# Neighbour sums with two matmuls per tile, eight-tile groups and 48 tiles per loop turn; locations on ScalarE's queue, t values added on GpSimd

## What is computed

```python
def sage(x, src, dst, W_l, b, W_r):
    summed = segment_sum(x[src], dst, N)
    deg = segment_sum(ones(E), dst, N)
    return (summed / maximum(deg, 1)[:, None]) @ W_l + b + x @ W_r

h = relu(sage(x, ..., W1_l, b1, W1_r))
x = x + sage(h, ..., W2_l, b2, W2_r)
```

## Time and profile before

| | us |
|---|---|
| time, median of 3 runs | 11395.62 |
| lowest and highest run | 11379.77, 11412.15 |
| span of the profiled execution | 11414.2 |
| PE, PEld busy | 6127.3 (54%), 4965.7 (44%) |
| DVE busy | 5543.8 (49%) |
| ACT busy | 2324.9 (20%) |
| POOL busy | 6528.7 (57%) |
| mean granted TensorE clock | 0.602 |

### The profile page before, as it was taken

One profiled execution on the slowest core, in us unless ns is written; L12 is line 12 of the kernel. 1 busy time (PEld: TensorE's weight loads), 2 busy tenths in 40 slices (PEclk: granted clock), 3 DMA queues, 4 the chain that ended last, 5 costly groups with the idle time before them and its releaser, 6 DMA issues. The chain is left out here.

```text
span 11414.2 us, 177920 instructions
## 1 busy us (share of the span) xinstructions
PE 6127.3 (54%) x45373; PEld 4965.7 (44%) x45374; DVE 5543.8 (49%) x10403; ACT 2324.9 (20%) x6224; POOL 6528.7 (57%) x6578
## 2 busy tenths in 40 slices
PE   5200066665777766666554646555555555554655
PEld 1100035553666664544444434334444444443444
DVE  9300075555555548888763536741111333383535
ACT  0000024442333321111004050011111111125050
POOL 0677737775677777777406060047777777756060
PEclk9555587787555558787556565565555555556565
DMA  9960012221433321111737475662000111126465
GB/s 367 199 61 5 14 44 84 82 83 50 117 102 101 100 73 51 53 54 49 145 94 246 84 261 127 140 52 27 13 13 8 27 28 28 25 53 255 98 252 104
DMA packets 1406964, 1074.85 MB, mean 94 GB/s; under 512 B 959771, under 2 KB 1258287, under 8 KB 1395302
## 3 DMA queue, kind: packets, MB, share of 16 engines
q1 hardware_dynamic: 1012260, 637.37, 24.3%
q0 software_dynamic: 239808, 283.02, 8.0%
q10 hardware_dynamic: 154752, 152.84, 4.4%
HBM read 553.89 MB, written 595.41 MB: 101 GB/s over the span
## 5 line engine op out<-in xcount | busy, mean ns | idle before, releaser
L2507 POOL DMA_INDIRECT msg<-msg,idx x1792 | 1743.1, 973 | 585.8 <-issue 531.7
L2337 POOL DMA_INDIRECT cell<-rec,idx x1008 | 1003.3, 995 | 1027.4 <-ACT rec L2325 737.0
L666 DVE TENSOR_TENSOR oh<-iota_f,rd 128x512 bf16<-128x512 f32 (+1 forms) x1261 | 824.8, 692 | 1379.1 <-PE ps L2259 1083.6
L979 POOL DMA_INDIRECT run_rows<-rec,idx x704 | 728.7, 1035 | 1274.7 <-ACT rec L962 1105.5
L2061 POOL DMA_INDIRECT cell<-rec,idx x1008 | 1073.6, 1065 | 421.3 <-issue 305.8
L1738 POOL DMA_INDIRECT rec_d<-rec,idx x880 | 907.2, 1031 | 453.8 <-issue 266.5
L397 POOL DMA_INDIRECT rec_r<-sc_rec,sc_idx x832 | 816.2, 981 | 596.5 <-ACT sc_rec L388 317.4
L2487 PE MATMUL ps<-w_stn,hft 128*128 x1792 | 600.1, 494 | 397.6 <-ACT hft L2441 389.6
L2274 PE MATMUL ps<-h_rows,oht 128*128 x2016 | 481.6, 403 | 583.3 <-ACT oht L2281 582.9
L1053 PE MATMUL ps<-got,oh 128*128 128x33 bf16 x12096 | 599.0, 197 | 334.7 <-DVE oh L666 319.0
L948 PE MATMUL ps<-planes,hot 128*128 x5632 | 493.2, 265 | 516.1 <-ACT rec L962 406.9
(11 more groups left out here) (416 smaller groups left out, 13529.0 us busy)
## 6 DMA issues: line engine op xcount, KB each, us to landing
loc<-loc_s SPq DMA_DIRECT2D x88, 2048.0 KB
got<-run_rows SPq DMA_DIRECT2D x1008, 112.0 KB
got<-rec_d SPq DMA_DIRECT2D x252, 416.0 KB
rec_d<-padd ACTq DMA_DIRECT2D x4, 13312.0 KB
rec_d<-padd ACTq DMA_DIRECT2D x4, 12896.0 KB
cell<-rec,idx POOLq DMA_INDIRECT x2016
loc<-loc_d SPq DMA_DIRECT2D x252, 128.0 KB
cin<-cell SPq DMA_DIRECT2D x224, 136.0 KB, 2.2
```

What stands on the lines that cost most here:

```text
L666: return nc.vector.tensor_tensor(oh, bcast(iota_f[:, :].unsqueeze(1), [P, G, P]), bcast(local.unsqueeze(2), [P, G, P]), ALU.is_equal)
L979: nc.gpsimd.indirect_dma_start(out=out, out_offset=bass.IndirectOffsetOnAxis(ap=idx[:, u, m % HU:m % HU + 1], axis=0), in_=rec[:, m, :], i ...
L2337: nc.gpsimd.indirect_dma_start(out=cells, out_offset=bass.IndirectOffsetOnAxis(ap=idx[:, n, g:g + 1], axis=0), in_=rec[:, n, g, :], in_off ...
L2507: nc.gpsimd.indirect_dma_start(out=msgs, out_offset=bass.IndirectOffsetOnAxis(ap=idx[:, n, g:g + 1], axis=0), in_=msg[:, n, g, :], in_offs ...
```

## The change

`sum_runs` is written anew with groups of GS = 8 tiles and RING = 6 buffers, so a turn has 48 tiles and there are 21 turns. The hi and mid planes lie side by side in a row, and one matmul of 66 columns takes both; a second of 33 adds lo to the first half. A block has 66 columns in PSUM, seven blocks to a bank, seven banks (`PER_BANK2`, `ABANKS2`), and the two halves are added when they are copied out. The addresses come from a new map `db`, made in `psum_address`, and are loaded 24 at a time, twice a turn. In the t pass the locations are loaded from ScalarE's queue when the pick six groups back is done; the pick stands in front of its own group's sum tiles and has one bank, 7; VectorE makes both one-hots three groups ahead and keeps only the here sum; GpSimd adds the three parts of t of the source side and both sides to the coordinates, four operations a group. `sort_sp` stores the map `db` without loading it; `source_runs` loads it. Parts that only rename or follow from this are cut.

```diff
+        def psum_address(then, c, tb, to, sets):
+
+            up = c["up"]
+            per, banks = (PER_BANK2, ABANKS2) if sets == 2 else (PER_BANK, ABANKS)
+            then(nc.vector.tensor_scalar(up[:, :], tb[:, :], float(per), None, ALU.is_ge))
+            for q in range(2, banks):
+                then(nc.vector.scalar_tensor_tensor(out=up[:, :], in0=tb[:, :], scalar=float(q * per), in1=up[:, :],
+                                                    op0=ALU.is_ge, op1=ALU.add))
+            then(nc.vector.tensor_scalar(up[:, :], up[:, :], float(512 - per * sets * AW), None, ALU.mult))
+            then(nc.vector.scalar_tensor_tensor(out=up[:, :], in0=tb[:, :], scalar=float(sets * AW), in1=up[:, :],
+                                                op0=ALU.mult, op1=ALU.add))
+            then(nc.vector.tensor_copy(to[:, :], up[:, :]))
...
+            elif tag == "r":
+                psum_address(then, c, tb, c["tba"], 2)
+            elif tag == "d":
+                psum_address(then, c, tb, c["tba"], 1)
+                psum_address(then, c, tb, c["tbb"], 2)
...
+            GS = 8
+            RING = 6
+            TURNS = TILES_D // (GS * RING)
+            HALF_TURN = RING // 2
+            K = TURNS * RING
+            PAIR = 2 * AW
...
-                        with sp.Fori(0, NID) as i:
-                            for n in range(R):
-                                k, t = i * R + n, i * STEP + n * G
+                        with sp.Fori(0, TURNS) as i:
+                            for n in range(RING):
+                                k = i * RING + n
                                 if planes is not None:
-                                    sp.wait_ge(s_node, k + 1)
-                                    sp.dma_start(loc[:, n, :], bcast(loc_d[ds(t * P, G * P)].unsqueeze(0), [P, G * P])).then_inc(s_loc[n], 16)
                                     sp.wait_ge(s_there, k + 1)
                                 sp.wait_ge(s_sum, k + 1)
-                                sp.dma_start(got[:, n, :, :], view[:, ds(t, G), :]).then_inc(s_got[n], 16)
+                                sp.dma_start(got[:, n, :, :], view[:, ds(k * GS, GS), :]).then_inc(s_got[n], 16)
...
+                        for q in range(ABANKS2):
+                            b0, nb = q * PER_BANK2, min(PER_BANK2, NB - q * PER_BANK2)
+                            nc.scalar.copy(table[:, q * 512:q * 512 + nb * PAIR].rearrange("p (b w) -> p b w", w=PAIR)[:, :, 0:12],
                                            planes[:, b0:b0 + nb, 3 * AW:3 * AW + 12]).then_inc(s_table, 1)
+                        with act.Fori(0, TURNS) as i:
+                            for n in range(RING):
+                                k = i * RING + n
+                                act.wait_ge(s_pick, k + 1)
+                                nc.scalar.dma_start(loc[:, n, :], bcast(loc_d[ds(k * GS * P, GS * P)].unsqueeze(0),
+                                                                        [P, GS * P])).then_inc(s_loc[n], 16)
...
-                            for g in range(G):
-                                mm = nc.tensor.matmul(ps[:, 6 + n % 2, g * 12:(g + 1) * 12], node_hot[:, n, g * P:(g + 1) * P],
-                                                      table[:, ds(at[g], 12)], start=True, stop=True)
-                            mm.then_inc(s_pick, 1)
...
+                        with pe.Fori(0, TURNS) as i:
+                            for n in range(RING):
+                                k, of = i * RING + n, n % HALF_TURN * GS
+                                if n % HALF_TURN == 0:
+                                    at = block_ids(ENG.PE, "db", k * GS, ABANKS2 * 512 - PAIR, HALF_TURN * GS)
+                                if planes is not None:
+                                    pe.wait_ge(s_node, k + 1)
+                                    pe.wait_ge(s_here, k + 1)
+                                    for g in range(GS):
+                                        mm = nc.tensor.matmul(ps[:, 7, g * 12:(g + 1) * 12],
+                                                              node_hot[:, n, g * P:(g + 1) * P], table[:, ds(at[of + g], 12)],
+                                                              start=True, stop=True)
+                                    mm.then_inc(s_pick, 1)
...
-                                for g in range(G):
-                                    for q in range(3):
-                                        mm = nc.tensor.matmul(sums[:, ds(at[n * G + g], AW)], oh[:, n, g, :], part[n][:, g, q * AW:(q + 1) * AW],
-                                                              start=False, stop=False)
+                                for g in range(GS):
+                                    nc.tensor.matmul(sums[:, ds(at[of + g], PAIR)], oh[:, n, g, :], part[n][:, g, 0:PAIR],
+                                                     start=False, stop=False)
+                                    mm = nc.tensor.matmul(sums[:, ds(at[of + g], AW)], oh[:, n, g, :], part[n][:, g, PAIR:PAIR + AW],
+                                                          start=False, stop=False)
...
+                        def hots(i, n):
+                            k = i * RING + n
+                            if planes is not None:
+                                v.wait_ge(s_loc[n], 16 * (i + 1))
+                                v.wait_ge(s_pick, k + 1)
+                                nc.vector.tensor_scalar(node_hot[:, n, :], loc[:, n, :], lane_c[:, 0:1], None, ALU.is_equal).then_inc(s_node, 1)
+                            v.wait_ge(s_sum, k + 1)
+                            nc.vector.tensor_tensor(oh[:, n, :, :], bcast(iota_f[:, :].unsqueeze(1), [P, GS, P]),
+                                                    bcast(rd[:, ds(k * GS, GS), LOC].unsqueeze(2), [P, GS, P]), ALU.is_equal).then_inc(s_hot, 1)
...
+                        def keep_here(i, n):
+                            k = i * RING + n
+                            v.wait_ge(s_pick, k + 1 + RING)
+                            v.wait_ge(s_with, k + 1)
+                            nc.vector.tensor_reduce(here[:, n, :, :],
+                                                    ps[:, 7, 0:GS * 12].rearrange("p (g q f) -> p g f q", g=GS, q=3)[:, :, 0:KD, :],
...
+                            AHEAD = 3
+
+                            def turn(i, last):
+                                for n in range(RING):
+                                    keep_here(i, n)
+                                    if not last or n + AHEAD < RING:
+                                        hots(i + (n + AHEAD) // RING, (n + AHEAD) % RING)
...
+                        for q in range(ABANKS2):
+                            nb = min(PER_BANK2, NB - q * PER_BANK2)
+                            nc.vector.tensor_copy(acc[:, q * PER_BANK2:q * PER_BANK2 + nb, :],
+                                                  ps[:, q, 0:nb * PAIR].rearrange("p (b w) -> p b w", w=PAIR)[:, :, 0:AW]).then_inc(s_kept, 1)
+                        for q in range(ABANKS2):
+                            nb = min(PER_BANK2, NB - q * PER_BANK2)
+                            to = acc[:, q * PER_BANK2:q * PER_BANK2 + nb, :]
+                            v.wait_ge(s_kept, q + 1)
+                            nc.vector.tensor_tensor(to, to, ps[:, q, 0:nb * PAIR].rearrange("p (b w) -> p b w", w=PAIR)[:, :, AW:PAIR],
+                                                    ALU.add).then_inc(s_kept, 1)
...
+                            for n in range(RING):
+                                k = i * RING + n
+                                new, att = (rd[:, ds(k * GS, GS), w:w + KD] for w in (NEWP, ATT))
+                                pool.wait_ge(s_got[n], 16 * (i + 1))
+                                pool.wait_ge(s_new, k + 1)
+                                nc.gpsimd.sem_inc(tick, 1)
+                                hi, mid, lo = (part[n][:, :, 3 * AW + 4 * q:3 * AW + 4 * q + KD] for q in range(3))
+                                nc.gpsimd.tensor_tensor(there[:, n, :, :], hi, mid, ALU.add).then_inc(s_part, 1)
+                                pool.wait_ge(s_part, k + 1 + RING)
+                                nc.gpsimd.sem_inc(tick, 1)
+                                nc.gpsimd.tensor_tensor(there[:, n, :, :], there[:, n, :, :], lo, ALU.add).then_inc(s_there, 1)
+                                pool.wait_ge(s_here, k + 2)
+                                nc.gpsimd.sem_inc(tick, 1)
+                                nc.gpsimd.tensor_tensor(new, here[:, n, :, :], att, ALU.add).then_inc(s_with, 1)
+                                pool.wait_ge(s_with, k + 1 + RING)
+                                pool.wait_ge(s_there, k + 1 + RING)
+                                nc.gpsimd.sem_inc(tick, 1)
+                                nc.gpsimd.tensor_tensor(new, new, there[:, n, :, :], ALU.subtract).then_inc(s_new, 1)
```

(2 more changed lines are left out.)

154 lines of the change are left out of this document (51 added, 103 removed).

## The result

The changed kernel takes **11179.13 us** (median of 5 runs, 11169.43 to 11236.53), the kernel before in the same session 11395.85 (5 runs). The ratio is 0.9823, with a 95% interval of 0.9807 to 0.9838: 217 us less by the medians. The forecast was 11166, 230 less.

What follows compares the result with a forecast made beforehand. TensorE's instruction queue was taken to bound the plain passes. Plain passes -117, t pass -141, ends +22, t pass start and end +4 and address map +2 gave -230 from 11395.6, so 11166 us; range 11110 to 11280.

Steps and rivals of the forecast that it cites:

- What bounds: Plain passes: TensorE's instruction queue sets the pace; a tile's address takes 0.115 us whether one matmul follows or three.
- The matmul rival: Sum passes: matmuls set the tile's step after all, so dropping one saves 109 us more, kernel 11057; chance 0.10.
- Plain passes, -117: Three plain sum passes: a turn of 10.25 us, 21 turns 215 us against 254.3, so -39 each.
- hand-over between groups: TensorE's queue: time from one group of tiles to the next, 0.12 us, worked out from a plain turn.
- The loop end: TensorE's queue: stops of 2.22 us for an address load at the loop end and 1.79 inside the body.
- The t pass, -141: Sum pass with t values: TensorE's queue next bounds it, 16.5 us a turn, 346 us against 487.3.
- GpSimd's cover: T pass: GpSimd's four dependent operations take 1.4 us a group, at most 2.3, below the 2.75 available.
- The rival with GpSimd as the bound: T pass: four GpSimd operations slowed beside VectorE take 3.1 us a group, pass 391, kernel 11211, or 11280; chance 0.36.
- Each meeting costs VectorE about 0.21: T pass: a VectorE two-input operation running beside GpSimd's takes about 0.21 us longer.
- Slower than before: T pass: every GpSimd operation waits out a whole one-hot, 6.7 us a group, +498, kernel 11664; chance 0.04.
- Ends, +22: Start and end of the four sum passes: more banks zeroed, closed and copied out, +5.4 us a pass.
- longer start: T pass: locations wait for the zeroing and GpSimd's last group comes behind, about +4 us.

Runs made afterwards that it cites:

- groups of four: Groups of 4 tiles in a ring of 12 instead of 8 in a ring of 6, against the changed kernel; 11331.0 us, 0.9954 of the kernel before.
- fixed columns: Changed kernel with sum matmuls writing to fixed columns instead of a register's address; 10903.9 us, 0.9581 of the kernel before.
- chain of eight: Changed kernel with GpSimd's first addition repeated four times, so eight dependent operations a group instead of four; 11328.9 us, 0.9957 of the kernel before.

## Why the prediction was right, and where its terms were off

Where the time of a pass goes can be read from TensorE's own queue. From one row's start to the next one's, summed between the first and the last sum matmul, in us:

| rows of the queue | plain, before | plain, after | t pass, before | t pass, after |
|---|---|---|---|---|
| address of a tile | 119.5 | 118.4 | 239.0 | 237.1 |
| register loads | 72.2 | 69.4 | 88.4 | 69.1 |
| waits between groups | 20.1 | 11.6 | 102.4 | 41.5 |
| other register rows | 11.6 | 4.2 | 23.2 | 4.2 |
| loop ends | 29.7 | 9.9 | 29.7 | 9.9 |

The columns add up to the passes, 253.1 and 213.5, 482.7 and 361.8. In the changed kernel nearly every row takes what others of its kind take, so hardly one of them stands waiting.

- **What bounds.** "The plain pass is bound by TensorE's instruction queue", by the address of each tile and not by its matmuls: shown by the runs with three and one matmul (no change) and by the run without addresses (73 us less in a plain pass). The matmul rival (chance 0.10) is out. The floor of the Trainium skill, TensorE: Matmul & The Clock Gate, section "Wait — 56ns, not 53.3ns?", doesn't bind in this kernel: by that page's 25 ns a dropped matmul would have given 101 us, by the runs it gives nothing.
- **Plain passes, -117:** measured -117.5. The turn was forecast as 10.25 us and is 10.28. The split was less exact. A hand-over between groups was put at 0.12 and is 0.105 by the groups of four; a tile was put at 0.115 and is 0.1175 on average, since some take 0.125 to 0.145. The two offset each other, because the 0.12 was what was left of the same total. The loop end, 2.22 - 1.79 = 0.43, is 0.36.
- **The t pass, -141:** measured -121.2; this is the term that was mis-sized. The failed step is "a group of 8 is 8 picks and 8 sum tiles at 0.115, and two hand-overs, 2.08 us". A group is 2.18 us: the picks of one group start at 7001.21 and of the next at 7003.39. The 0.12 of a hand-over came from the plain pass, where it is one row. In the t pass the two are three rows, 41.5 us a pass instead of 126 x 0.24 = 30. The tiles, two steps for each, take 237 instead of 232, and the stops 1 us less than forecast. That is the 16 us between 362 and the 346 of the forecast. The other 4 of the 20 are in what the forecast set the 346 against: 487.3 before, where first to last sum matmul take 483. With one of the three rows taken away the pass is 349 us.
- **GpSimd's cover.** "At most 4 x (0.40 + 0.18) = 2.3" was too low: it is 2.5 of 2.87 us, though the third operation needs no hand-over from the second. The conclusion held (with GpSimd idle the pass takes the same), but with 0.37 us of slack a group where the forecast counted on 0.45 to 1.35. "Below 2.75, if nothing holds them up" named the gap: about one of the four is held by the sum one-hot, and often one by the node one-hot. The rival with GpSimd as the bound (0.36) was nearer than the numbers of the sum made it; groups of four bring it in, and so do fixed columns.
- **VectorE beside GpSimd.** "Each meeting costs VectorE about 0.21": measured 1.255 against 1.219 for a one-hot, 0.036. The GPSIMD Engine Reference of the Trainium skill, Key points, states that GpSimd contends with VectorE's operations of two inputs. The trace agrees for GpSimd, whose 24-column operation takes 0.23 us clear of the two-input one-hot and ends only behind it where it starts under it. VectorE itself hardly loses.
- **Slower than before (0.04).** "Each operation stopped by the whole of a one-hot" is what happens, but to about one operation of a group, not to all four: the ones behind it come after the one-hot has ended. So the chain of eight takes 4.06 us a group, still below the 4.6 from which the forecast let it decide, and its kernel is at 0.9957.
- **Ends, +22:** measured 4.35, 4.3 and 4.2 in the plain passes. In the t pass only the end grew, by 3.3; together +16. The "longer start" (+4) is not there: from the zeroing of its operand on VectorE to the first sum matmul the t pass takes 6.83 us before and 6.81 after, and GpSimd's last operation ends 0.44 us behind the last sum matmul's start. The sum by stages is -117.5 - 121.2 + 16 = -223, and the medians give -217; the address map (+2) was not measured apart. So the total came nearer to the forecast than the t pass did, in part by offsetting errors: the t pass gained 20 us less than forecast, and ends and start cost 10 less.
- **Where the gain comes from.** The names in the change mislead: two matmuls for three, the locations' queue and GpSimd are each worth nothing within what the runs tell. By the table the plain pass gains 20 us by fewer loop ends, 8.5 by fewer waits between groups, 7 by fewer register rows and 3 by fewer loads: 39.6 of 39.9 with the tiles. The t pass gains 61 us by its waits, the true ones for VectorE among them, 20 by loop ends, 19 by loads and 19 by register rows.

## What to carry to other kernels

When an engine's queue sets the pace, count the rows that queue has to issue: here 0.115 us a tile with a register's address, 0.064 us an address loaded, 0.26 us a load, 0.10 us for each row that a wait leaves even when it is met, 0.36 us a loop end. The engine's own work (matmuls, columns) may then change freely, up to the next bound. Of a change that does several things, undo each alone before believing the one it is named for. Before giving small dependent operations to GpSimd, count VectorE's long operations that they will meet, not their own number: here an operation of 0.23 us took about 1.0 for each sum one-hot met.

## What the runs showed that was not expected

- A GpSimd addition of 24 columns takes 0.23 us, but one that starts while VectorE makes a sum one-hot ends only 0.09 to 0.10 us behind it, 103 of 103 times. That made about 0.95 us a group for a chain of four and for one of eight.
- A wait already met costs TensorE's queue as much as most of a tile where it leaves a row: 0.100 against 0.115 us.
- Without the address the tile's step was 0.084 us, close to that of its 99 columns at 1.2 GHz: the address was only a good third above it.
